# A gated two-layer block on one core: transposes of the selection counts go from TensorE to DMA, and the turn from one chunk to the next is laid out anew

## What is computed

```python
xn = layernorm(x)
s  = xn @ (block_masked(weight)).T + bias                 # 512 -> 512
inter = xn @ c1_w.T @ c2_w.T                              # rank 16, 1792 columns
idx = argmax(inter.reshape(rows, 56, 32), -1) + 32 * arange(56)
h   = relu(w1[idx] . xn)                                  # one of each 32 hidden units counts
g   = silu(sum over idx of h * w2t[idx])                  # 1792 -> 512
x   = x + s * g
```

## Time and profile before

| | us |
|---|---|
| time, median of 3 runs | 694.86 (693.66 to 695.56) |
| time of the profiled execution | 693.95 |
| its span, first to last instruction | 692.2 |
| TensorE busy | 659.1 (95%) |
| VectorE busy | 457.0 (66%) |
| ScalarE busy | 214.4 (31%) |
| GpSimd busy | 231.7 (33%) |
| rank product of chunks 1, 2, 3 begins at | 128.84, 230.98, 333.14 |
| layer 1 begins at | 440.12 |

### The profile page before, as it was taken

The page is one execution under the profiler, slowest core; times in us unless marked ns, Lnnn a source line. Parts: engine busy times, 40 slices in busy tenths (PEclk is TensorE's granted clock), DMA queues, the critical chain, the costliest instruction groups (busy, mean ns, idle before and its releaser), DMA issues.

```text
span 692.2 us, 8636 instructions
## 1 busy us (share of the span) xinstructions
PE 659.1 (95%) x3078; PEld 518.1 (75%) x3078; DVE 457.0 (66%) x715; ACT 214.4 (31%) x379; POOL 231.7 (33%) x185
## 2 busy tenths in 40 slices
PE   2699999999999999999999999989999999999997
PEld 2577777877787777787777777657877877787787
DVE  7877775596665596665597776674856566485543
ACT  3424343312222412222312233443145125313610
POOL 1516455450000540000661226433514242341441
PEclk9899999999999999999999999999999999999999
DMA  8940000040000130000152110040031013002001
GB/s 235 386 166 1 0 1 0 32 152 1 0 1 0 47 136 0 0 0 0 45 207 80 58 62 0 32 153 0 31 110 43 1 45 136 0 30 91 2 16 46
DMA packets 19535, 40.66 MB, mean 59 GB/s; under 512 B 2032, under 2 KB 2416, under 8 KB 18864
## 3 DMA queue, kind: packets, MB, share of 16 engines
q1 hardware_dynamic: 19504, 40.25, 16.8%
HBM read 31.85 MB, written 8.39 MB: 58 GB/s over the span
## 4 chain that ended last, share of the span: by engine, by line
PE 84%; DVE 10%; issue 3%; DMA 1%; ACT 1%; POOL 0%; SPq 0%; DVEq 0%; ACTq 0%
PE bank L404 74%; PE bank L338 2%; PE bank L1141 2%; DVE eq L862 2%; PE bank L1236 2%; DVE seg_top L860 1%; PE bank L1104 1%; PE bank L1122 1%; DVE counts L872 1%; PE bank L1273 1%; DVE h_lo L896 1%; DVE ws_lo L925 1%; DMA x_tile<-in_x 1%; DVE x_tile L378 1%; DVE h L887 0%
## 5 line engine op out<-in xcount | busy, mean ns | idle before, releaser
L404 PE MATMUL bank<-w_hi_t,h_hi 128*128 128x512 f32 x224 | 93.7, 418 | 1.7 <-DVE h_lo L896 1.7
L698 ACT ACTIVATE h_hi<-h 128x512 fp32r<-128x512 f32 x56 | 35.4, 632 | 182.8 <-DVE h L887 182.8
L872 DVE TENSOR_TENSOR_SCAN counts<-restart,eq 128x512 bf16<-128x512 bf16 (+1 forms) x64 | 88.3, 1380 | 2.1
L404 PE MATMUL bank<-xT_hi,w_hi_t 128*128 128x512 f32 x224 | 88.9, 397 | 0.0
L404 PE MATMUL bank<-w_hi_t,h_lo 128*128 128x512 f32 x224 | 88.5, 395 | 0.0
L404 PE MATMUL bank<-w_lo_t,h_hi 128*128 128x512 f32 x224 | 88.5, 395 | 0.0
L404 PE MATMUL bank<-xT_hi,w_lo_t 128*128 128x512 f32 x224 | 88.5, 395 | 0.0
L404 PE MATMUL bank<-xT_lo,w_hi_t 128*128 128x512 f32 x224 | 88.4, 395 | 0.0
L860 DVE TENSOR_REDUCE seg_top<-bank 128x16 f32<-128x512 f32 (+1 forms) x64 | 39.5, 618 | 72.7 <-PE bank L1122 72.7
L384 POOL TENSOR_TENSOR g_tile<-g_tile,s_tile 128x512 f32<-128x512 f32 x31 | 40.6, 1311 | 95.2 <-DVE g_tile L909 56.4
L612 POOL TENSOR_TENSOR prod_lo<-prod,prod_hi 128x512 fp32r<-128x512 f32 x32 | 40.7, 1292 | 74.4 <-ACT prod_hi L736 74.4
(11 more groups left out here) (184 smaller groups left out, 1326.2 us busy)
## 6 DMA issues: line engine op xcount, KB each, us to landing
w_raw<-in_w SPq DMA_DIRECT2D x28, 256.0 KB, 10.1
x_res<-in_x SPq DMA_DIRECT2D x4, 1024.0 KB, 8.2
mid_state<-g_tile SPq DMA_DIRECT2D x16, 256.0 KB, 2.1
x_tile<-mid_state SPq DMA_DIRECT2D x4, 1024.0 KB, 7.6
x_res<-mid_state SPq DMA_DIRECT2D x4, 1024.0 KB, 5.6
out<-g_tile SPq DMA_DIRECT2D x15, 256.0 KB, 2.0
x_tile<-in_x SPq DMA_DIRECT2D x3, 1024.0 KB, 5.4
b_raw<-in_lora_b SPq DMA_DIRECT2D x2, 1024.0 KB, 4.9
```

Of the source, the lines that this page charges most:

```text
L404: last = nc.tensor.matmul(dst, a, b, start=(start and n == 0), stop=(stop and n == len(mms) - 1))
L698: nc.scalar.activation(h_hi[:, it % 2, :], h[:], ACT.Copy).then_inc(h_hi_done, 1)
L872: nc.vector.tensor_tensor_scan(counts[:, p % 2, tt, 0:PW[p]], restart[:, 0:PW[p]], eq[:, 0:PW[p]], 0.0, ALU.mult, ALU.add).then_inc(sel_co ...
```

## The change

- **Counts by DMA.** `transpose_counts` on TensorE goes. In its place ScalarE issues, for each of the 16 selections, one `dma_start_transpose` from `counts` (now one piece, [128, 4, 512]) to a new buffer `first` in SBUF, [128, 2, 4, 512] in bf16, two pieces deep (`turn_counts`). It stands on ScalarE in the head after each `s_read`, after ReLU of it = 1, and after `h_hi` of it = 1 to 11. VectorE waits for the four transposes of a piece at it = 0, 4, 8 and 12, and its mask now reads `first` and `h` both from SBUF. A count waits for the DMA that reads its buffer's last contents.
- **Two selection banks.** Bank 7 is free and becomes the second of `sels`; a selection waits for the one two before it.
- **Two buffers of h.** ReLU of it waits for `h_split` of it - 2.
- **The turn of a chunk.** The next chunk's rows are transposed in one go, behind `down(11)`, into banks 7, 6, 0 and 1. Then `down(12)`, half of `down(13)`, the rank product of the next chunk, and the other half of `down(13)`. The head is then selection and s product in turn, four times, with no wait for rows. On ScalarE and VectorE the first two row splits stand within it = 13, and `t_round` and `t_rest` before tanh and silu.
- **The gate** on GpSimd makes the four products first and then the four sums.

```diff
-        counts = span_t.take("counts", [P, 2, TT, BANK], BF16)
+        first = span_t.take("first", [P, 2, TT, S], BF16)
+        counts = span_t.take("counts", [P, TT, BANK], BF16)
-        h = span_t.take("h", [P, S])
+        h = span_t.take("h", [P, 2, S])
...
-            return banks[(0, 1, 6, 0)[tt]] if isinstance(g, int) and g == 0 else banks[tt % 2]
+            return banks[tt % 2] if l1 else banks[(7, 6, 0, 1)[tt]]
...
+            def turn_counts(c, p, tt):
+
+                act.wait_ge(sel_count, c * NSEL + p * TT + tt + 1)
+                if p >= 2:
+                    act.wait_ge(h_masked, c * IT + 4 * (p - 1))
+                elif not (isinstance(c, int) and c == 0):
+                    act.wait_ge(h_masked, c * IT)
+                act.sem_inc(turns, 1)
+                act.dma_start_transpose(first[:, p % 2, 0:PW[p] // P, rows(tt)], counts[:, tt, 0:PW[p]])\
+                    .then_inc(ld_first[tt], 16)
+
             def head(c):
-                t_round(c)
                 for tt in range(TT):
                     s_read(c, tt)
+                    turn_counts(c, 0, tt)
...
                     act.wait_ge(up_done, c * IT + it + 1)
-                    if it:
-                        act.wait_ge(h_split, c * IT + it)
-                    nc.scalar.activation(h[:], up[it % 2][:], ACT.Relu).then_inc(relu_done, 1)
+                    if it >= 2:
+                        act.wait_ge(h_split, c * IT + it - 1)
+                    nc.scalar.activation(h[:, it % 2, :], up[it % 2][:], ACT.Relu).then_inc(relu_done, 1)
+                    if it == 1:
+                        turn_counts(c, 1, 0)
...
+                    if 0 < it < 4 * (PIECES - 1):
+                        turn_counts(c, it // 4 + 1, it % 4)
...
-                    dve.wait_ge(first_tr, c * IT + it + 1)
-                    nc.vector.scalar_tensor_tensor(h[:], first, 1.0, h[:], ALU.is_equal, ALU.mult).then_inc(h_masked, 1)
+                    if it % 4 == 0:
+                        for tt in range(TT):
+                            dve.wait_ge(ld_first[tt], (c * PIECES + it // 4 + 1) * 16)
+                    nc.vector.scalar_tensor_tensor(h[:, it % 2, :], first[:, it // 4 % 2, it % 4, :], 1.0, h[:, it % 2, :],
+                                                   ALU.is_equal, ALU.mult).then_inc(h_masked, 1)
...
             def head(c):
-                pe.wait_ge(xT_done, c * TT + TT)
-                rank_product()
-                s_product(c, 0)
-                s_product(c, 1)
-                select(c, 0, 0)
-                s_product(c, 2)
-                select(c, 0, 1)
-                s_product(c, 3)
-                select(c, 0, 2)
+                for tt in range(TT):
+                    select(c, 0, tt)
+                    s_product(c, tt)
...
-                    transpose_counts(c, it - 1)
...
+                pe.wait_ge(sel_eq, c * NSEL + NSEL)
+                for tt in range(2):
+                    transpose_rows(pe, c + 1, tt)
+                pe.wait_ge(relu_done, c * IT + IT - 1)
+                transpose_rows(pe, c + 1, 2)
                 pe.wait_ge(relu_done, c * IT + IT)
-                transpose_rows(pe, c + 1, 1)
-                pe.wait_ge(xT_done, (c + 1) * TT + 1)
-                transpose_rows(pe, c + 1, 2)
+                transpose_rows(pe, c + 1, 3)
+                pe.wait_ge(h_split, c * IT + IT - 1)
+                down_product(IT - 2, range(TT)).then_inc(down_done, 1)
                 pe.wait_ge(h_split, c * IT + IT)
                 down_product(IT - 1, range(0, 2))
-                pe.wait_ge(xT_done, (c + 1) * TT + 2)
-                transpose_rows(pe, c + 1, 3)
+                if not last:
+                    pe.wait_ge(xT_done, (c + 1) * TT + TT)
+                    rank_product()
                 down_product(IT - 1, range(2, TT)).then_inc(down_done, 1)
```

More of the change, by code:

```diff
@@ L263, in block_mask_ffn_then_attention_lora_kernel @@
         sel_count = sem("sel_count")
-        first_tr = sem("first_tr")
+        turns = sem("turns")
+        ld_first = [sem(f"ld_first_{tt}") for tt in range(TT)]
         up_done = sem("up_done")
@@ L410, in block_mask_ffn_then_attention_lora_kernel @@
         on = g_tile[:, 0, 2 * P:3 * P]
-        c2_f = counts[:].bitcast(F32).rearrange("p a t n -> p (a t n)")[:, 0:INTER]
+        c2_f = first[:].bitcast(F32).rearrange("p a t n -> p (a t n)")[:, 0:INTER]
         C2_PARTS = [slice(0, BANK), slice(BANK, INTER)]
@@ L414, in block_mask_ffn_then_attention_lora_kernel @@
         acc = [banks[2 + tt] for tt in range(TT)]
-        sel = banks[6]
+        sels = [banks[6], banks[7]]
         mask_bank = banks[5]
-        first = banks[7][:].bitcast(BF16)[:, 0:S]
         NSEL = PIECES * TT
@@ L686, in body @@
                             w2_round(1)
-                            for tt in range(TT):
-                                s_read(c, tt)
+                            head(c)
                         if it + 4 < IT:
@@ L697, in body @@
                         act.wait_ge(down_done, c * IT + it - 1)
-                    nc.scalar.activation(h_hi[:, it % 2, :], h[:], ACT.Copy).then_inc(h_hi_done, 1)
-                for tt in range(TT):
+                    nc.scalar.activation(h_hi[:, it % 2, :], h[:, it % 2, :], ACT.Copy).then_inc(h_hi_done, 1)
+                    if 0 < it < 4 * (PIECES - 1):
+                        turn_counts(c, it // 4 + 1, it % 4)
+                for tt in range(2, TT):
                     rows_hi(act, c + 1, tt)
+                if not last:
+                    t_round(c + 1)
                 act.wait_ge(down_done, c * IT + IT)
@@ L903, in body @@
                         rows_norm(dve, c + 1)
-                for tt in range(TT):
+                for tt in range(2, TT):
                     rows_lo(dve, c + 1, tt)
+                if not last:
+                    t_rest(c + 1)
                 for tt in range(TT):
@@ L927, in _ @@
             dve.wait_ge(c2_split, 2)
-            for tt in range(TT - 1):
-                select(0, 0, tt)
+            head(0)
             body(0, False)
@@ L1103, in rank_product @@
                     for x in (xT_hi, xT_lo):
-                        last = nc.tensor.matmul(sel[:], c1_stack[:, k, :], x[:, k, :], start=(k == 0 and x is xT_hi),
+                        last = nc.tensor.matmul(sels[0][:], c1_stack[:, k, :], x[:, k, :], start=(k == 0 and x is xT_hi),
                                                 stop=(k == KD - 1 and x is xT_lo))
@@ L1115, in select @@
             def select(c, p, tt):
-                if p == 0 and tt == 0:
+                n = p * TT + tt
+                if n == 0:
                     pe.wait_ge(t_split, c + 1)
-                else:
-                    pe.wait_ge(sel_eq, c * NSEL + p * TT + tt)
-                nc.tensor.matmul(sel[:, 0:PW[p]], t_stack[:, rows(tt)],
+                elif n >= 2:
+                    pe.wait_ge(sel_eq, c * NSEL + n - 1)
+                nc.tensor.matmul(sels[n % 2][:, 0:PW[p]], t_stack[:, rows(tt)],
                                  c2_stack[:, p * BANK:p * BANK + PW[p]], start=True, stop=True).then_inc(sel_done, 1)
@@ L1133, in up_product @@
                                       for k in range(KD)]).then_inc(up_done, 1)
-            def transpose_counts(c, it):
-                pe.wait_ge(sel_count, c * NSEL + (it // 4 + 1) * TT)
-                if it:
-                    pe.wait_ge(h_masked, c * IT + it)
-                for tt in range(TT):
-                    last = nc.tensor.transpose(first[:, rows(tt)], counts[:, it // 4 % 2, tt, rows(it % 4)], ident_bf[:])
-                last.then_inc(first_tr, 1)
             def down_product(it, tts):
@@ L1152, in head, with body @@
             def head(c):
-                pe.wait_ge(xT_done, c * TT + TT)
-                rank_product()
-                s_product(c, 0)
-                s_product(c, 1)
-                select(c, 0, 0)
-                s_product(c, 2)
-                select(c, 0, 1)
-                s_product(c, 3)
-                select(c, 0, 2)
-            def body(c, first):
+                for tt in range(TT):
+                    select(c, 0, tt)
+                    s_product(c, tt)
+            def body(c, first, last):
                 if not first:
                     up_product(c, 0)
-                    select(c, 0, 3)
-                for it in range(1, IT + 1):
-                    if it < IT:
-                        if not (first and it == 1):
-                            up_product(c, it)
-                        if (it - 1) // 4 + 1 < PIECES:
-                            select(c, (it - 1) // 4 + 1, (it - 1) % 4)
-                    else:
-                        pe.wait_ge(relu_done, c * IT + IT - 1)
-                        transpose_rows(pe, c + 1, 0)
-                    transpose_counts(c, it - 1)
+                for it in range(1, IT):
+                    if not (first and it == 1):
+                        up_product(c, it)
```

(2 more changed lines are left out.)

67 lines of the change are left out of this document (38 added, 29 removed).

## The result

The changed kernel takes 704.59 us (median of 4, 700.60 to 710.68) against 694.26 us of the kernel before, beside it: a ratio of 1.0154, with a 95% interval of 1.0095 to 1.0214. The forecast was 690.3 with a range of 683.5 to 709. The time lies in the range, the sign is the other one.

What follows compares the result with a forecast made beforehand. TensorE, 95% busy, bounds the kernel. Removals of 20.2 us less costs given back left 0 in chunk 0, -3.7 in chunks 1 and 2, -0.85 in chunk 3: 693.95 - 4.55 = 689.4, plus 0.9 for the median, 690.3; range 683.5 to 709.

Steps and rivals of the forecast that it cites:

- What is taken out: TensorE's stream: count transposes, a selection wait and breaks removed, 5.35 us in chunks 1 to 3, 4.2 in chunk 0.
- T = 2.9: Time of one DMA transpose from its start on ScalarE to landing: estimated 2.9 us, 1.6 of it issue.
- The slow rival: DMA transposes take 5.0 us each, near a 1 MB load; kernel at 707 us; chance 0.20.
- The collision: Heads of chunks 1 to 3: loads of x issued just before the fourth transpose slow it by 0.4 us.
- a rival with a chance of 0.12: Fourth transpose of a head queues behind 2 MB of loads, 6.3 us in three heads: 697 us; chance 0.12.
- Chunk 0, 0.5 us for masks beside the splits: Body of chunk 0: VectorE's masks beside GpSimd's weight splits cost 0.5 us.
- The head without a collision, 2.6 us: Heads of chunks 1 to 3: 2.3 us given back before `down(0)`, 0.3 for `s_read`s behind transposes.
- The end, 0.5 us: End of each chunk: TensorE waits 0.5 us before the row transposes, as the mask of it = 12 needs the last transposes.
- Chunk 3's end: Before the last row transposes, normalizing beside GpSimd's splits: wait about 4.2 us in place of 2.7, 1.0 more for chunk 3.

Runs made afterwards that it cites:

- The run at T = 0: Changed kernel without its 64 DMA transposes and turned counts, masks reading fixed positions from a constant tile: 679.21 us, ratio 0.9797.
- late loads: Changed kernel with each chunk's 2 MB loads of x issued only after VectorE's mask of it = 0: 691.27 us, ratio 0.9968.
- the mask from PSUM: On late loads: for it >= 2 the mask reads the up product from PSUM without ScalarE's ReLU, and comes ahead of the selection: 697.77 us.
- the version that won: On late loads: PSUM masks except at it = 0, 1, 4, 8, 12, VectorE reordered, `wqkv` split one it later: 679.16 us, ratio 0.9795.
- filler: Changed kernel with 13 useless matmuls (11 in chunk 0) ahead of `down(0)`'s wait in chunks 0 to 2: 705.79 us.
- the head's new order: On late loads: in heads ScalarE issues each transpose one `s_read` later and ReLU of it = 0 ahead of the fourth: 693.47 us.

## Why the prediction was wrong

- **What is taken out, 5.35 us a chunk: right in the middle chunks.** The run at T = 0 has them at 96.8 and 97.0, 5.1 to 5.4 less than 102.16. Over the kernel it is 14.6 us and not 20.2, as chunks 0 and 3 gain little.
- **T = 2.9: nearly right**, 2.4 measured, with 1.2 and not 1.6 of it on ScalarE. The slow rival (T = 5), to which I gave the largest chance of all rivals, was wrong. So was the estimate of 5.2 us, four times the 1309 ns for a square on the Trainium skill's page "VectorE: DVE Perf Modes" (The three transpose paths): the trace has 2.4 us for four squares, issue included. The Trainium skill's page "Advanced Engine Details and Errata" (X-Bar Transpose (TRN2)), by which transposing DMAs are as fast as regular ones, is nearer: 2.4 beside 1.7 for a store of the same bytes.
- **The collision, 0.4 us a head: the step that failed.** I priced it as fair sharing of bandwidth and put the real thing into a rival with a chance of 0.12. The trace shows 3.4 us of wait in a middle head, the transposes landing with the loads though issued before them. The rival's own price (T = 5.4 there, 6.3 us for three heads) was too low as well: T came to 6.1 to 6.4, and I had no term for the lower clock after the wait, 1.55 and 2.3 us in the two middle chunks. Moving the loads gave back 13.3. How the engines shared their time between the two queues stays open. The page counts 30720 packets for the 7.35 MB of transposes and 19504 for the 40.25 MB of the other queue, 0.24 and 2.1 KB each, so sharing by turns of packets would favour the loads, but no run tested that.
- **Chunk 0, 0.5 us for masks beside the splits: the second that failed.** I had the row for it, `h_lo` at 1.80 with SBUF inputs beside GpSimd, and used it once in the head, halved, but took 0.5 for 14 masks in the body. Each costs 0.95 more (1.61 against 0.66), VectorE falls behind TensorE, and the splits come to some 5.7 us in the body.
- **The head without a collision, 2.6 us: too much.** With late loads `up(2)` waits 0.5 and `down(0)` 0.4. VectorE's last count came 16.7 us after the last down product (17.2 forecast), T was 0.3 shorter, and 0.7 of contention hit the mask and not `h_lo`.
- **The end, 0.5 us: not there** in middle chunks. The first normalized tile is ready 1.3 us sooner than I counted, from an issue 0.5 sooner, T 0.5 shorter and shorter handovers. Chunk 3's end has waits of 1.68, 0.69 and 0.84 us, 3.2 in place of 2.7, where I had 4.2.

With the collision away the kernel takes 691.3, near the forecast of 690.3. That is luck and no merit of the sum: chunk 0 is 4.0 us worse than I said, and each middle chunk 2 us better.

## What to carry to other kernels

Before moving a small transfer to the DMA engines, look up what large transfers are issued within its own duration, ahead *and behind* it, on any queue (here 0.8 us behind was too close and 0.9 was not); where they can wait, tie them to an event after the small one's consumer. Where an operand moves from PSUM to SBUF, multiply by the count of uses, not once, wherever GpSimd works beside. And where a wait moves, ask what buffer the waiting instruction releases: the mask from PSUM was faster and still lost; in the version that won, those few that wait for a DMA kept their copy.

## What the runs showed that I had not expected

- A DMA transpose of 128x512 2-byte elements occupies the issuing engine for 1.2 us (1.18 to 1.21 in the rows above; a plain issue 0.41).
- Issued 0.46 us ahead of 2 MB of plain loads on another queue, it lands after 6.2 us; with the loads 4.2 us behind it, after 2.6, and in chunk 3 with them 0.9 behind it after 2.5 (0.81: 5.6).
- After TensorE's waits of 2.65, 2.75, 3.25 and 3.45 us in the changed kernel the granted clock fell to its lower level (1.2 GHz), at once or up to four matmuls later, for 7 to 13 steps of 0.43 us in place of 0.233. After 2.17 us, with the row transposes in between, six steps were slow. Where filler kept TensorE at work it didn't fall. The length of the wait alone doesn't tell: the same wait in chunk 3 was followed by eight slow steps in the changed kernel and by none with late loads (the row below, clock 1.00 behind it). In the run with masks from PSUM waits of 2.96 and 3.12 brought none, while in the run with the head's new order nine slow steps followed three waits of 1.69, 0.69 and 0.72.

```profile
381.34 0.50 PE L414 MATMUL bank<-w_hi_t,h_hi 128*128 128x512 f32 x1 [2.75 <-DVE h_lo L931]
```

- Beside GpSimd's subtractions VectorE's operations with two SBUF inputs take longer: mask 1.61 us against 0.69 in a middle chunk, `ws_lo` 5.70 against 2.50, scan 2.04 against 1.22, and one scan of chunk 3 4.45. Masks, maxima and comparisons that read PSUM take 0.66 to 0.69 in either case.
